# A Mamba block and a binarized feed-forward on one core: decay factors first in each chunk, shifts of the norms on GpSimd, the feed-forward norm on ScalarE, statistics at other places, one bank place skipped

## The chip, the cores and the metric

The kernel runs on one core of a Trainium2 chip. The metric is the device time of one execution in microseconds (us). A core has four compute engines with a queue of instructions each, executed in order: TensorE (PE in the rows), VectorE (DVE), ScalarE (ACT) and GpSimd (POOL). SyncE (SP) issues the DMAs. The engines wait for each other with semaphores only.

## The reference

The input is 8 sequences (batches) of 1024 tokens with 256 features. All in float32:

```
x = x + layernorm(ssd(layernorm(x)))
x = x + layernorm(ffn(layernorm(x)))

ssd:  x, z = in @ Wx.T, in @ Wz.T                    (256 -> 512)
      x = silu(causal_conv(x, 4 taps) + conv_b)
      b, c = x @ Wb.T, x @ Wc.T                      (512 -> 8 heads of 64)
      dt = softplus(x @ Wdt.T + b_dt);  a = -exp(log_a)
      state = exp(dt*a)*state + dt*b (outer) x;  y = c . state     (over 1024 tokens)
      y = y + d_param * x
      yn = (y - mean) / sqrt(var + eps) * gn_w + gn_b   (mean, var per head, over all 1024 tokens)
      out = (yn * silu(z)) @ Wout.T                  (512 -> 256)
ffn:  h = gelu(in @ bw1.T + b1);  out = h @ bw2.T + b2   (256 -> 1024 -> 256)
      bw = mean(|w|) per row * sign(w)
```

## The kernel before

**Staging.** Each batch is two halves (`j` = 0, 1) of 512 tokens, and a half is four chunks (`q` = 0 to 3) of 128. The recurrence is done chunk by chunk. Since the head norm needs the mean over all 1024 tokens, the rest of a batch (head norm, Wout, feed-forward: the "tail") can start only when its second half is through. It is then done inside the next batch: a turn of the loop holds a batch's own steps, the tail of the batch before, and the first steps of the next one.

**Order.** `turn_steps` (from line 147) is one list of steps that all engines share. Each engine walks down the list and issues what the step means for it; steps without a handler on an engine are passed over. So the list sets the order in every queue. After the last batch, `last_tail` orders what is left.

**A half in steady state.** TensorE does the x projection (`xi`), the z projection (`z`), the Wout product of the batch before (`Wo`), then `B`, `dt`, `C` interleaved with the feed-forward of the batch before (`uT` turns its input, `H` is the first layer in eight parts), and then four chunks. VectorE does the convolution and splits float32 tensors into two float16 parts (high part by ScalarE, low part by VectorE: `xh`, `sh`, `uh`, `hh`).

**A chunk** has these steps. `ends`: a matmul gives the decay exponents (key `E`), ScalarE takes the exponential into `Cd`, GpSimd multiplies by `C` (line 814). `front`: exponents of the decay matrix (`seg`), turned x and B (`X`, `Bt`), VectorE makes `xdt` and GpSimd `xdw` (line 807). `score`: C times B, masked by VectorE (`mt`, line 1238). `carry`: the new part of the state (`St`, line 1616) and what the old state gives to y (line 1625); GpSimd scales the state (line 825), VectorE adds to it (line 1244). `back`: the rest of y (line 1638), added by VectorE to `yT` (line 1254). Of the tail, the chunks also carry the second feed-forward layer (`O`), the last norm and the store.

**Norms.** A row norm is: statistics on VectorE (`statistics`, lines 1082 to 1091), 1/sqrt on GpSimd as a power (line 759), and then either one VectorE pass (`normal`, line 1097: the "mid" and "ff" norms) or a shift -mean*rstd on VectorE (line 1109) and a ScalarE pass (line 894: "in" and "end"). The head norm's scale and shift are applied by ScalarE (line 1041, step `gate`); the gate product is VectorE's in the first half and GpSimd's (line 791) in the second. Both `gate` steps of the second half stand in the first half of a turn, behind the step `ff_norm`.

**Banks.** Five of the eight PSUM banks go round among a batch's own products in the order of the list (`Ring`): a matmul waits until the product five places earlier has been read. Two banks serve the tail, one the turned input and the running sums. Every batch starts the round anew at bank 0.

## Time and profile before

| | us |
|---|---|
| median of 3 runs | 1361.92 (1361.39 to 1361.99) |
| profiled execution, its own time | 1363.99 |
| its span, first to last instruction | 1362.2 |
| TensorE / VectorE / ScalarE / GpSimd busy | 92% / 76% / 61% / 34% |
| one turn in steady state | 159.5 |
| mean granted TensorE clock | 0.98 |

The span leaves 1.8 us of the execution's own time outside. One turn is the distance between two equal matmuls a batch apart (483.35 and 642.85 us). A row of the timeline has its start, its length, the engine, the line, the operation with its tensors, and in brackets the idle time before it with the engine that ended it.

### The profile page before, as it was taken

The page shows a single profiled execution, that of the slowest core. Times are in us where ns is not written, and L with a number is a line of the kernel's source. Part 1 is how long each engine was busy: PE and PEld are TensorE (multiplying, and loading weights), DVE is VectorE, ACT ScalarE, POOL GpSimd, SP SyncE. Part 2 cuts the span into 40 slices and gives each one's busy share as a digit, 9 for nine tenths or more (in the row PEclk, how much of TensorE's full clock was granted, in tenths as well). Part 3 has the DMA queues.
Part 4 walks back from the last instruction along what each step waited for, and adds up shares of the span by engine and source line. Part 5 has one row for each costly group of instructions (what it writes and reads, how often), then busy time and mean ns, then how long its engine had stood idle before and what let it go on. Part 6 is the DMA issues. An engine that isn't in the chain of part 4 may idle for free.

```text
span 1362.2 us, 28268 instructions
## 1 busy us (share of the span) xinstructions
PE 1253.5 (92%) x10744; PEld 800.6 (59%) x10744; DVE 1039.2 (76%) x2432; ACT 831.6 (61%) x1432; POOL 458.4 (34%) x527
## 2 busy tenths in 40 slices
PE   6999899999999999999998999999999999989675
PEld 3564657566565756656575665757556475756543
DVE  4664787878879797878978787796977788787574
ACT  5664675657755585656856577565856568565433
POOL 2030433323351334315333243513343153332533
PEclk9998999999999999999999999999999999999888
DMA  7010000101000010100101010010101000000000
GB/s 221 1 48 1 17 0 2 47 1 48 1 18 32 2 47 1 48 1 17 32 2 47 1 48 0 3 47 2 47 2 48 1 2 32 2 32 1 32 1 31
DMA packets 30565, 32.91 MB, mean 24 GB/s; under 512 B 1856, under 2 KB 28628, under 8 KB 30432
## 3 DMA queue, kind: packets, MB, share of 16 engines
q1 hardware_dynamic: 30432, 31.11, 7.1%
q8 instruction: 86, 1.41, 0.4%
q14 instruction: 47, 0.39, 0.1%
HBM read 22.72 MB, written 8.39 MB: 23 GB/s over the span
## 4 chain that ended last, share of the span: by engine, by line
PE 49%; DVE 19%; issue 14%; POOL 12%; ACT 5%; POOLq 0%; DVEq 0%; ACTq 0%
PE bank L1490 21%; PE bank L1675 8%; PE bank L1660 4%; PE bank L1688 4%; DVE xs L1125 4%; POOL Cd L814 3%; PE bank L1602 2%; POOL xdw L807 2%; DVE un L1097 2%; PE bank L1580 2%; DVE hh L1304 2%; DVE gn_stats L1261 1%; POOL state L825 1%; PE bank L1529 1%; POOL y L777 1%
## 5 line engine op out<-in xcount | busy, mean ns | idle before, releaser
L814 POOL TENSOR_TENSOR Cd<-Cd,CT 128x512 f32<-128x512 f32 x64 | 81.2, 1269 | 360.5 <-ACT Cd L1033 360.0
L1490 PE MATMUL bank<-sh,WbT 128*128 128x512 f16 x768 | 177.8, 385 | 12.4 <-DVE sh L1130 12.4
L1490 PE MATMUL bank<-sh,WcT 128*128 128x512 f16 x768 | 175.9, 379 | 0.0
L1490 PEld LDWEIGHTS bank<-sh,WbT 128*128 128x128 f16 x768 | 72.9, 99 | 103.7 <-DVE sh L1130 22.1
L1125 DVE SCALAR_TENSOR_TENSOR xs<-xi,vectors,xs 128x512 f32<-128x512 f32 x168 | 125.2, 749 | 4.5 <-ACT xs L938 0.8
L1490 PEld LDWEIGHTS bank<-sh,WcT 128*128 128x128 f16 x768 | 75.1, 98 | 86.6
L1675 PE MATMUL bank<-uh,sign1T 128*128 128x512 f16 x512 | 121.8, 383 | 2.5 <-DVE uh L1332 2.5
L1062 ACT ACTIVATE hf<-bank,vectors,alpha 128x512 f32<-128x512 f32 x128 | 99.6, 778 | 39.2 <-PE bank L1675 28.0
L1688 PE MATMUL bank<-sign2T,hh 128*128 128x256 f16 x1024 | 119.0, 275 | 1.8 <-DVE hh L1345 1.8
L999 ACT ACTIVATE CT<-bank 128x512 f32<-128x512 f32 x64 | 38.1, 595 | 134.1 <-PE bank L1490 134.1
L1688 PEld LDWEIGHTS bank<-sign2T,hh 128*128 128x128 f16 x1024 | 99.6, 99 | 19.0 <-issue 4.3
L1023 ACT ACTIVATE mt<-bank 128x512 f32<-128x512 f32 x128 | 69.6, 599 | 60.9 <-PE bank L1572 60.9
L1490 PE MATMUL bank<-xh,WxT 128*128 128x512 f16 x384 | 90.5, 388 | 13.5 <-DVE state L1244 13.5
L1343 DVE TENSOR_SCALAR hh<-hf 128x512 f16<-128x512 f32 x128 | 54.4, 425 | 58.4 <-ACT hf L1062 57.9
L1238 DVE TENSOR_TENSOR mt<-bank,mt 128x512 f32<-128x512 f32 x128 | 82.2, 684 | 16.0 <-PE bank L1602 16.0
L759 POOL TENSOR_TENSOR rstd_mid<-var_eps_mid,power 128x4 f32<-128x4 f32 x16 | 16.5, 1034 | 230.7 <-DVE var_eps_mid L1091 230.7
L1345 DVE SCALAR_TENSOR_TENSOR hh<-hf,hh 128x512 f16<-128x512 f32 x128 | 89.0, 695 | 4.4
L807 POOL TENSOR_TENSOR xdw<-xdt,decays 128x512 f32<-128x512 f32 x64 | 66.7, 1042 | 71.5 <-DVE xdt L1229 71.5
L1033 ACT ACTIVATE Cd<-bank 128x512 f32<-128x512 f32 x64 | 38.1, 596 | 83.1 <-PE bank L1591 82.5
L1490 PE MATMUL bank<-xh,WzT 128*128 128x512 f16 x384 | 87.3, 384 | 0.0
L1675 PEld LDWEIGHTS bank<-uh,sign1T 128*128 128x128 f16 x512 | 49.3, 99 | 61.0 <-issue 4.9
L1602 PE MATMUL bank<-CT,BT 64*128 64x128 f32 x1024 | 75.0, 286 | 1.6 <-ACT mt L1023 1.6
(207 smaller groups left out, 2682.4 us busy)
## 6 DMA issues: line engine op xcount, KB each, us to landing
xt<-L_attn_input_tensor_dram SPq DMA_DIRECT2D x16, 512.0 KB, 5.0
u<-L_attn_input_tensor_dram SPq DMA_DIRECT2D x16, 512.0 KB, 4.0
out_dram<-u SPq DMA_DIRECT2D x16, 512.0 KB, 3.0
yT<-in_L_ffn_w_dram SPq DMA_DIRECT2D x2, 512.0 KB, 9.6
u<-in_L_ffn_w_dram SPq DMA_DIRECT2D x2, 512.0 KB, 9.5
BT<-in_L_attn_Wx_dram SPq DMA_DIRECT2D x1, 512.0 KB, 4.8
BT<-in_L_attn_Wz_dram SPq DMA_DIRECT2D x1, 512.0 KB, 5.7
zs<-in_L_attn_Wb_dram SPq DMA_DIRECT2D x1, 512.0 KB, 5.6
```

Of the source, the lines that this page charges most:

```text
L807: pool.tensor_tensor(xdw[n % 2][:, :, :], xdt[n % 2][:, :, :], per_head(to_end[:, q, :]), ALU.mult)\
L814: pool.tensor_tensor(Cd[n % 2][:, :, :], Cd[n % 2][:, :, :], CT[:, :, q * P:(q + 1) * P], ALU.mult)\
L1023: nc.scalar.activation(mt[n % 2][:, g].rearrange("p c t -> p (c t)"), bank(t, ("seg", j, q, g))[:, :], ACT.Exp).then_inc(seg_exp.sem, 1)
L1062: nc.scalar.activation(hf[f % 2][:, :], bank(t, ("H", j, f))[:, :], ACT.Gelu, bias=b1_col[:, f:f + 1], scale=alpha1[:, f:f + 1]).then_inc( ...
L1125: nc.vector.scalar_tensor_tensor(out=conv_sum(j, c), in0=xi[:, c, k:k + BLK], scalar=taps[:, c, k:k + 1], in1=conv_sum(j, c), op0=ALU.mult ...
L1238: nc.vector.tensor_tensor(v, bank(t, ("S", j, q, g))[:, :], v, ALU.mult).then_inc(mt_out.sem, 1)
L1345: nc.vector.scalar_tensor_tensor(out=hh[1][:, f, :], in0=hf[f % 2][:, :], scalar=SG, in1=hh[0][:, f, :], op0=ALU.mult, op1=ALU.subtract).t ...
L1490: mm = nc.tensor.matmul(bank(t, key)[:, :], w[i][:, k, cols(m)], v[h][:, k, :], start=(a == 0), stop=(a == len(terms) - 1))
L1602: mm = nc.tensor.matmul(bank(t, key)[:, cols(c)], BT[rows, c, cols(q)], CT[rows, c, cols(q)], start=True, stop=True)
L1660: mm = nc.tensor.matmul(bank(t, key)[:, (i % 2) * D:(i % 2 + 1) * D], yT[:, c, (j * NQ + i) * P:(j * NQ + i + 1) * P], WoutT[:, c, :], sta ...
L1675: mm = nc.tensor.matmul(bank(t, key)[:, :], sign1T[:, k, cols(f)], uh[i][:, k, :], start=(a == 0), stop=(a == len(terms) - 1))
L1688: mm = nc.tensor.matmul(bank(t, key)[:, (i % 2) * D:(i % 2 + 1) * D], hh[p][:, f, cols(i)], sign2T[:, f, :], start=(a == 0), stop=(a == le ...
```

## The change

Seven things change.

1. In a chunk, `ends` of chunk q+1 stands ahead of its `front` (before: behind the `carry` of chunk q).
2. The shift of a norm is computed by GpSimd right behind the power, from -mean, which VectorE now writes. The feed-forward norm gets a shift too.
3. The feed-forward norm's pass moves from VectorE to ScalarE. Only the first batch's input norm moves the other way.
4. The input norm's statistics move from the first chunk to behind `H` 1; its pass moves to behind the first `front`, and the first turning (`xT` 0) ahead of the second `O`.
5. The head statistics of tokens 0 to 255 move from the end of the first half to the second half, behind `H` 3.
6. `end_root` (1/sqrt of the last norm) moves ahead of `ends`, `front` and `score` of the last chunk.
7. In the ring of five banks one place is left empty ahead of the last `carry` of a batch.

```diff
@@ class Ring
+        self.keys = [key for key in keys if key is not None]
...
+            if key is None:
+                continue
@@ turn_steps
-        steps += own(("C", j, 0), ("cums", j)) + tail(("uT", j)) + own(("roles", j), ("skip", j), ("C", j, 1)) + tail(("H", j, 0), ("H", j, 1))
+        steps += own(("C", j, 0), ("cums", j)) + tail(("uT", j)) + own(("roles", j), ("skip", j), ("C", j, 1))
+        steps += tail(("H", j, 0), ("H", j, 1)) + [(who, "in_stat", nj)]
...
-        steps += own(("C", j, 2)) + tail(("H", j, 2), ("H", j, 3))
+        steps += own(("C", j, 2)) + tail(("H", j, 2), ("H", j, 3)) + (own(("head_stat", 0, 0)) if j else [])
...
-        steps += own(("decays", j), ("ends", j, 0), ("front", j, 0)) + [(who, "in_stat", nj)] + tail(("O", j, 0))
+        norm, xT = [(who, "in_norm", nj)], [[(who, "xT", nj, k)] for k in range(KD)]
+        steps += own(("decays", j), ("ends", j, 0), ("front", j, 0)) + ([] if first else norm) + tail(("O", j, 0))
...
-        steps += own(("score", j, 0), ("front", j, 1))
+        steps += own(("score", j, 0), ("ends", j, 1), ("front", j, 1))
...
-        steps += own(("score", j, 1))
-        norm = [(who, "in_norm", nj)]
-        steps += own(("carry", j, 0), ("ends", j, 1)) + (own(("back", j, 0)) + norm if first else norm + tail(("O", j, 1)) + own(("back", j, 0)))
-        steps += own(("front", j, 2)) + [(who, "xT", nj, 0)] + own(("score", j, 2), ("carry", j, 1), ("ends", j, 2))
-        steps += [(who, "xT", nj, 1)] + own(("back", j, 1)) + tail(("end_stat", j)) + own(("front", j, 3), ("score", j, 3)) + tail(("end_root", j))
+        steps += own(("score", j, 1), ("carry", j, 0)) + ([] if first else xT[0]) + tail(("O", j, 1)) + own(("back", j, 0))
+        steps += (norm if first else []) + own(("ends", j, 2), ("front", j, 2)) + (xT[0] if first else [])
+        steps += own(("score", j, 2), ("carry", j, 1)) + xT[1] + own(("back", j, 1)) + tail(("end_stat", j), ("end_root", j))
+        steps += own(("ends", j, 3), ("front", j, 3), ("score", j, 3))
         steps += [(who, "xi", nj, 0)] if j else []
         steps += own(("head_stat", 1, 0)) if j else []
-        steps += own(("carry", j, 2), ("ends", j, 3)) + tail(("end_norm", j, 0), ("end_norm", j, 1)) + own(("back", j, 2))
+        steps += own(("carry", j, 2)) + tail(("end_norm", j, 0), ("end_norm", j, 1)) + own(("back", j, 2))
...
-        steps += [(who, "silu_table")] + own(("carry", j, 3), ("back", j, 3)) + ([] if j else own(("head_stat", 0, 0)))
+        steps += [(who, "silu_table")] + own(("carry", j, 3), ("back", j, 3))
@@ the ring's keys
+            if (who, kind, *at) == ("own", "carry", NJ - 1, NQ - 1):
+                own_keys.append(None)
@@ GpSimd, inverse_root
+                    if w in ln_shift:
+                        pool.wait_ge(*ln_rstd[w].count(t, j + 1))
+                        pool.tensor_tensor(ln_shift[w][:, :], minus_mean[w][:, :], rstd[w][:, :], ALU.mult)\
+                            .then_inc(ln_shifts[w].sem, 1)
@@ ScalarE
+            def ff_norm(t, j):
+                for i in range(NQ):
+                    normal("ff", un, u[j], t, j, i)
@@ VectorE, statistics
+                    nc.vector.tensor_scalar(minus_mean[w][:, :], moments[w][:, :, 0], -1.0, None, ALU.mult)
...
-                nc.vector.scalar_tensor_tensor(out=ln_shift[w][:, :], in0=moments[w][:, :, 0], scalar=-1.0,
...
-            def ff_norm(t, j):
-
-                for i in range(NQ):
-                    normal("ff", t, j, un[:, i, :], u[j][:, i, :], i).then_inc(un_out.sem, 1)
```

**ScalarE, first half of a turn.** `table_in` is the loading of the gelu table, `un` the feed-forward norm's output, `yT` with `gn_scale` the head norm of the second half, `CT` the first C product copied out of its bank, `cum_hi` the running sums' high part, `uh` the turned feed-forward input. Before:

```order
L890 ACTIVATE table_in<-ones 128x1
L1041 ACTIVATE yT<-yT,gn_shift,gn_scale 128x256 x8
L999 ACTIVATE CT<-bank 128x512
L1006 ACTIVATE cum_hi<-bank 128x128
L1057 ACTIVATE uh<-bank 128x512 x2
```

The same place with the change:

```order
L901 ACTIVATE table_in<-ones 128x1
L905 ACTIVATE un<-u,ln_shift_ff,rstd_ff 128x256 x4
L1056 ACTIVATE yT<-yT,gn_shift,gn_scale 128x256 x8
L1014 ACTIVATE CT<-bank 128x512
L1021 ACTIVATE cum_hi<-bank 128x128
L1072 ACTIVATE uh<-bank 128x512 x2
```

Four passes have come in ahead of the eight head-norm passes, and these stand ahead of `CT` and `uh` as before.

**GpSimd, the last two chunks of a half.** `Cd` are the end factors times C, `xdw` the weighted x, `state` the scaling of the state, `rstd_end` and `ln_shift_end` belong to the last norm, `u0` is the sum that is stored. Before:

```order
L807 TENSOR_TENSOR xdw0<-xdt0,decays 128x512
L825 TENSOR_TENSOR state<-state,decays 128x256
L814 TENSOR_TENSOR Cd0<-Cd0,CT 128x512
L807 TENSOR_TENSOR xdw1<-xdt1,decays 128x512
L759 TENSOR_TENSOR rstd_end<-var_eps_end,power 128x4
L825 TENSOR_TENSOR state<-state,decays 128x256
L814 TENSOR_TENSOR Cd1<-Cd1,CT 128x512
L825 TENSOR_TENSOR state<-state,decays 128x256
L782 TENSOR_TENSOR u0<-u0,y2 128x256 x4
```

The same place with the change:

```order
L825 TENSOR_TENSOR Cd0<-Cd0,CT 128x512
L818 TENSOR_TENSOR xdw0<-xdt0,decays 128x512
L836 TENSOR_TENSOR state<-state,decays 128x256
L766 TENSOR_TENSOR rstd_end<-var_eps_end,power 128x4
L770 TENSOR_TENSOR ln_shift_end<-minus_mean_end,rstd_end 128x4
L825 TENSOR_TENSOR Cd1<-Cd1,CT 128x512
L818 TENSOR_TENSOR xdw1<-xdt1,decays 128x512
L836 TENSOR_TENSOR state<-state,decays 128x256 x2
L793 TENSOR_TENSOR u0<-u0,y2 128x256 x4
```

`rstd_end` now stands ahead of both `Cd1` and `xdw1` of the last chunk, and the scaling of the state behind all of them.

**VectorE, from the end of the first half into the second.** `hh` with `yT` is the gated output's low part, `gn_stats` the head statistics, `xs` with `xi` the convolution, `sh` the low part of its result. Before:

```order
L1254 TENSOR_TENSOR yT<-bank,yT 128x2x128 x2
L1261 BN_STATS gn_stats<-yT 128x6 x4
L1304 SCALAR_TENSOR_TENSOR hh<-yT,hh 128x512 x2
L1125 SCALAR_TENSOR_TENSOR xs<-xi,vectors,xs 128x512 x3
L1261 BN_STATS gn_stats<-yT 128x6 x4
L1125 SCALAR_TENSOR_TENSOR xs<-xi,vectors,xs 128x512 x6
L1130 SCALAR_TENSOR_TENSOR sh<-xs,sh 128x512
```

The same place with the change:

```order
L1266 TENSOR_TENSOR yT<-bank,yT 128x2x128 x2
L1316 SCALAR_TENSOR_TENSOR hh<-yT,hh 128x512 x2
L1137 SCALAR_TENSOR_TENSOR xs<-xi,vectors,xs 128x512 x3
L1273 BN_STATS gn_stats<-yT 128x6 x4
L1137 SCALAR_TENSOR_TENSOR xs<-xi,vectors,xs 128x512 x6
L1142 SCALAR_TENSOR_TENSOR sh<-xs,sh 128x512
```

Four statistics instructions have left the stretch ahead of the convolution.

## Rows read from the trace of the kernel before

**Rows 1.** The page's first part: busy time, share of the span, instructions.
```profile
PE 1253.5 (92%) x10744; PEld 800.6 (59%) x10744; DVE 1039.2 (76%) x2432; ACT 831.6 (61%) x1432; POOL 458.4 (34%) x527
```

**Rows 2.** TensorE's waits, whole run: total us, times, longest.
```profile
PE bank L1625 <- DVE yT L1254: 20.2, 14, 1.8
PE bank L1490 <- DVE state L1244: 13.5, 12, 1.8
PE bank L1490 <- DVE sh L1130: 12.4, 15, 1.9
...
PE bank L1500 <- ACT xt L894: 3.9, 7, 2.7
...
PE bank L1625 <- POOL Cd L814: 1.5, 2, 0.8
```

**Rows 3.** Timeline, feed-forward norm in the first half: start, length, [idle before].
```profile
507.51 4.03 ACT L1041 ACTIVATE yT<-yT,gn_shift,gn_scale 128x256 f32<-128x256 f32 x8
...
511.39 1.02 POOL L759 TENSOR_TENSOR rstd_ff<-var_eps_ff,power 128x4 f32<-128x4 f32 x1 [2.81 <-DVE var_eps_ff L1091]
...
512.44 3.01 DVE L1097 TENSOR_SCALAR un<-u,moments_ff,rstd_ff 128x256 f32<-128x256 f32 x4 [0.53 <-POOL rstd_ff L759]
...
514.24 0.60 ACT L999 ACTIVATE CT<-bank 128x512 f32<-128x512 f32 x1 [2.71 <-PE bank L1490]
...
514.74 0.27 ACT L1006 ACTIVATE cum_hi<-bank 128x128 f16<-128x128 f32 x1
...
515.87 1.08 ACT L1057 ACTIVATE uh<-bank 128x512 f16<-128x512 f32 x2 [0.87 <-PE bank L1500]
...
516.50 1.29 DVE L1332 TENSOR_TENSOR uh<-bank,uh 128x512 f16<-128x512 f32 x2 [0.19 <-ACT uh L1057]
...
518.70 1.89 PE L1675 MATMUL bank<-uh,sign1T 128*128 128x512 f16 x8
```

**Rows 4.** Timeline, the same norm in the second half.
```profile
592.78 1.38 DVE L1097 TENSOR_SCALAR un<-u,moments_ff,rstd_ff 128x256 f32<-128x256 f32 x4 [0.53 <-POOL rstd_ff L759]
...
594.17 1.04 PE L1500 MATMUL bank<-ident,un 128*128 128x128 f32 x8
```

**Rows 5.** Timeline, last two chunks of a first half.
```profile
555.17 0.17 DVE L1091 TENSOR_SCALAR var_eps_end<-moments_end 128x4 f32<-128x4 f32 x1
...
556.05 1.04 POOL L807 TENSOR_TENSOR xdw<-xdt,decays 128x512 f32<-128x512 f32 x1 [3.37 <-DVE xdt L1229]
...
557.05 1.02 POOL L759 TENSOR_TENSOR rstd_end<-var_eps_end,power 128x4 f32<-128x4 f32 x1
...
558.04 0.61 POOL L825 TENSOR_TENSOR state<-state,decays 128x256 f32<-128x256 f32 x1
558.61 1.26 POOL L814 TENSOR_TENSOR Cd<-Cd,CT 128x512 f32<-128x512 f32 x1
...
559.92 2.08 ACT L894 ACTIVATE y<-y,ln_shift_end,rstd_end 128x256 f32<-128x256 f32 x4 [2.26 <-DVE ln_shift_end L1109]
560.33 0.67 PE L1625 MATMUL bank<-Cd,state 64*64 64x128 f32 x16 [1.81 <-DVE yT L1254]
```

**Rows 6.** Timeline, a GpSimd instruction of 128x4 that is no power.
```profile
1.50 0.10 POOL L734 MEMSET power<- 128x4 f32 x1
```

**Rows 7.** Timeline: B in batch 0, x projection after a second half, B later.
```profile
109.91 4.05 PE L1490 MATMUL bank<-sh,WbT 128*128 128x512 f16 x9 [1.94 <-DVE sh L1130]
...
483.35 4.06 PE L1490 MATMUL bank<-xh,WxT 128*128 128x512 f16 x18 [1.76 <-DVE state L1244]
...
579.78 0.82 PE L1490 MATMUL bank<-sh,WbT 128*128 128x512 f16 x3 [0.80 <-DVE sh L1130]
```

**Rows 8.** Timeline, first feed-forward layer of two halves in the last tail.
```profile
1310.23 8.75 PE L1675 MATMUL bank<-uh,sign1T 128*128 128x512 f16 x32 [2.47 <-DVE uh L1332]
...
1332.49 7.07 PE L1675 MATMUL bank<-uh,sign1T 128*128 128x512 f16 x32
```

**Rows 9.** Stretch of TensorE alone: us, busy, granted clock, DMA share, GB/s.
```profile
1310.00:1314.00 4.00, 3.77 (x10) 0.57 0.00 0
```

More of the change, by code:

```diff
@@ L354, in mamba_sandwich_kernel @@
         rstd = {w: sb(f"rstd_{w}", [P, NQ]) for w in LNS}
-        ln_shift = {w: sb(f"ln_shift_{w}", [P, NQ]) for w in ("in", "end")}
+        ln_shift = {w: sb(f"ln_shift_{w}", [P, NQ]) for w in ("in", "ff", "end")}
+        minus_mean = {w: sb(f"minus_mean_{w}", [P, NQ]) for w in ln_shift}
         gn_stats = sb("gn_stats", [P, KI, NJ * 2, 6])
@@ L482, in mamba_sandwich_kernel @@
         ln_rstd = {w: Signal(sem(f"ln_rstd_{w}"), NJ) for w in LNS}
-        ln_shifts = {w: Signal(sem(f"ln_shifts_{w}"), NJ) for w in ("in", "end")}
+        ln_shifts = {w: Signal(sem(f"ln_shifts_{w}"), NJ) for w in ln_shift}
         xn_made = Signal(sem("xn_made"), NJ * NQ)
@@ L540, in mamba_sandwich_kernel @@
         o_out = Signal(sem("o_out"), NJ * NQ)
-        normed = {"in": xn_made, "end": y2_norm}
+        normed = {"in": xn_made, "ff": un_out, "end": y2_norm}
         def ffn_buffer(t, j):
@@ L890, in table, with normal @@
                 return lambda t: nc.scalar.activation(table_in[:, :], ones[:, 0:1], func)
[L892 removed]
+            def normal(w, out, v, t, j, i):
                 act.wait_ge(*ln_shifts[w].count(t, j + 1))
[L894 removed]
+                nc.scalar.activation(out[:, i, :], v[:, i, :], ACT.Identity, bias=ln_shift[w][:, i:i + 1],
                                      scale=rstd[w][:, i:i + 1]).then_inc(normed[w].sem, 1)
             def input_norm(t, j):
+                for i in range(0 if opening(t) else NQ):
+                    normal("in", xt[j], xt[j], t, j, i)
+            def ff_norm(t, j):
                 for i in range(NQ):
[L899 removed]
+                    normal("ff", un, u[j], t, j, i)
             def end_norm(t, j, m=None):
                 for i in range(NQ) if m is None else range(2 * m, 2 * m + 2):
[L903 removed]
+                    normal("end", ffn_buffer(t, j), ffn_buffer(t, j), t, j, i)
             def input_high(t, j, k):
@@ L1102, in input_stats, with input_norm @@
                            lambda i: dve.wait_ge(*x_in[j].count(t, 1)) if i == 0 else None)
-            def shift(w):
-                def step(t, j, m=0):
-                    if m:
-                        return
-                    dve.wait_ge(*ln_rstd[w].count(t, j + 1))
-                    nc.vector.scalar_tensor_tensor(out=ln_shift[w][:, :], in0=moments[w][:, :, 0], scalar=-1.0,
-                                                   in1=rstd[w][:, :], op0=ALU.mult, op1=ALU.mult).then_inc(ln_shifts[w].sem, 1)
-                return step
+            def input_norm(t, j):
+                for i in range(NQ if opening(t) else 0):
+                    normal("in", t, j, xt[j][:, i, :], xt[j][:, i, :], i).then_inc(xn_made.sem, 1)
             def input_low(t, j, k):
@@ L1412, in _ @@
                 "gn_fold": head_fold, "gate": gate, "gated": gated_low, "mid_stat": middle_stats, "mid_norm": middle_norm,
-                "ff_stat": ff_stats, "ff_norm": ff_norm, "uT": middle_low, "H": hidden_split, "O": ffn_out,
-                "end_stat": end_stats, "end_norm": shift("end")}
+                "ff_stat": ff_stats, "uT": middle_low, "H": hidden_split, "O": ffn_out,
+                "end_stat": end_stats}
             dve.wait_ge(masks_made, MASKS_MADE)
```

18 lines of the change are left out of this document (7 added, 11 removed).

## The prediction

> **What bounds the kernel now.** I read the page's busy shares first [rows 1]. TensorE is busy 92% of the span, VectorE 76%, and TensorE goes through the same work every 159.5 us. So what counts is TensorE's idle time, and an edit is worth what it takes from that or adds to it. Next come TensorE's waits [rows 2]. Three stand out: the last chunk's old-state product waits for VectorE's addition into `yT` (20.2 us in 14 halves, up to 1.81 [rows 5]); the x projection waits for VectorE's state addition (13.5; 1.76 after each second half [rows 7]); B waits for the low part `sh` (12.4). They add up to 46 us, and that is about the most that the change can win. Last I followed the timeline around each moved step.
>
> **1. The feed-forward norm on ScalarE, first half.** Before, ScalarE does eight head-norm passes from 507.51 to 511.54, in time in which it has nothing else to do, and then idles 2.71 us until C's first bank is full at 514.24 [rows 3]. Now the four norm passes stand ahead of these eight. They need the shift, which comes after the power that ends at 512.41. With -mean on VectorE (0.1) and the shift (0.2, below) they start at about 512.8. Four passes take 2.08 us [rows 5], the eight 4.03, the copy of C 0.5 to its successor, `cum_hi` 0.27 and the two copies of `uh` 1.08 [rows 3]. The copies end at 512.8 + 2.1 + 4.05 + 0.5 + 0.27 + 1.08 = 520.8. VectorE's low part ended 0.84 behind ScalarE (517.79 against 516.95), so 521.65, and the hidden layer starts at 521.8 instead of 518.70: +3.1 us. TensorE meanwhile has only the turning of `un` and one C product, which were through at 518.70 before and would be a little earlier now, since ScalarE's last pass ends at 514.9 and VectorE's ended at 515.45. So it stands idle for over 3.1, some 3.5 us in one piece. Seven turns: +21.7.
>
> **2. The clock after that idle time.** Before the hidden layer of the last tail TensorE idles 2.47 us; the 32 matmuls then take 8.75 us, where the same 32 take 7.07 at full speed [rows 8], and the granted clock of that stretch is 0.57, so most of it ran at 1.2 instead of 2.4 GHz [rows 9]. After the 1.81 us waits nothing of the kind shows: that product has its usual 0.67 [rows 5]. A pause of 3.5 us lies beyond the 2.47. I take the measured 1.68 each time, seven times +11.8. Bounds 0 and 1.7.
>
> **3. The same norm, second half.** No head-norm passes stand in the way. VectorE needed 1.38 us for the four parts and TensorE began to turn them at 594.17 without a wait [rows 4]. ScalarE takes 2.08 and starts about 0.3 later (-mean, shift), so the last part is there at 595.3 and the turning ends 0.8 later. +0.8 seven times: +5.6. In the first half VectorE's passes took 3.01 us [rows 3], beside GpSimd's gate products; that gain is in part 1, where it only makes the pause longer.
>
> The Trainium skill (VectorE: DVE Perf Modes, "Mode 2×_2P — use both read ports for one tensor") says that a float32 operation with one tensor source in SBUF runs two elements per cycle on VectorE, which speaks against moving this pass. By that rule VectorE's four passes are the cheaper ones; the rows (1.38 against 2.08) agree, and the sum has their difference already.
>
> **4. The shift on GpSimd.** No row shows a small product on GpSimd. Below it lies a memset of the same 128x4 at 0.10 [rows 6], above it the power at 1.02 [rows 5]. I take 0.2 with its wait, near the memset, since the scaling of a whole 128x256 state takes only 0.61. VectorE loses its own shift between the state addition and the addition into `yT`.
>
> The Trainium skill (GPSIMD Engine Reference, "2.1 Instruction dispatch") gives an indirect call of tens of cycles per instruction; an estimate from that page is under 0.1 us, and the sum would be lower by about 2 us.
>
> **5. End of a half.** The wait of 1.81 does not go, it changes its reason. GpSimd's queue before: `xdw` (1.04), power (1.02), state (0.61), `Cd` [rows 5]. Now: power, shift, `Cd` (1.26), `xdw` (1.04), state. The queue starts when the variance is there (555.34 before; 555.7 now, with one more small VectorE operation in front, a slightly later start and the semaphore), so state scaling runs at 555.7 + 1.02 + 0.25 + 1.27 + 1.04 = 559.3 to 559.9 instead of 558.04 to 558.65. VectorE adds until 560.4, and the product that started at 560.33 starts at 560.5. Queued behind `Cd` is `xdw` of the last chunk, needed by the last `St`, which waits for it until 559.3 too, inside the same pause. In the second half it is the same with head statistics in between: about +0.3 for VectorE's state and `yT` additions. The early `ends` adds another thing: in chunk 1, `X` now comes five places behind the first `score` bank and waits for VectorE's mask, 0.1 us a half. Fourteen halves: +1.4 for both together.
>
> **6. What really goes.** After the first half VectorE is ahead: the last norm's pass starts on ScalarE some 2.5 us earlier (at 557.0 instead of 559.92 [rows 5]), hence also the gated output, and the head statistics of four instructions are gone from here. Of the x projection's 13.5, six waits of 1.76 are 10.6 and the first batch has some 0.8; the rest, 2.1, lies after first halves and goes: -2.1. The waits of B in second halves go too: of the 12.4 some 5.1 are the first batch's, whose waits are the long ones (1.94 [rows 7]) and stay; -7.3. After the second half the skipped place frees the first x product of the 1.76 wait, but its second one takes the bank of `St`, whose reader is the same state addition behind the convolution, and then the head means wait for statistics that come 0.3 later. I give it -0.2 in six turns, -1.2; bounds 0 and -10.6.
>
> **7. First batch and last tail.** Without a tail, the early end factors and early norm work as meant: of the waits for `xt` (3.9), for `Cd` (1.5) and one of 0.8 for the state I let 5.8 go, -5.8. In the last tail one ScalarE norm and two shifts lie open: +1.0.
>
> The statistics of the input norm go into VectorE's pauses between the hidden parts; they take some 2.2 us a half (four statistics, four aggregates, two small operations); VectorE is not what TensorE waits for there, and if the pauses did not hide them, the hidden parts would come up to 2.2 later in a half, before a second layer that starts only after the first `front`. The DMAs wait for the same steps as before.
>
> **Sum.** 21.7 + 11.8 + 5.6 + 1.4 - 2.1 - 7.3 - 1.2 - 5.8 + 1.0 = +25.1. On the profiled execution (1362.2 of span and 1.8 around it, 1364.0) that is 1389.1; this one is 2.1 above the median of the runs, so for a run like those it is 1361.9 + 25.1 = 1387.
>
> **Rivals.**
> A. The pause does not pull the clock down, or only in part. For it: the pause sits between dense matmuls, while the last tail is thin anyway. Against it: [rows 8, 9]. 1387 - 11.8 = 1375. Chance 0.15.
> B. A small GpSimd product costs nearly what the power costs, 0.8 more than I took. It lies in both feed-forward norms and both ends of a half, four times a turn: +22, 1409. For it: every 128x4 operation between tensors there has 1.02. Chance 0.08.
> C. Faster: the ends of the halves come free. If the variance of the last norm reaches GpSimd before the last chunk's `Cd` and `xdw` are wanted, the state chain runs as early as TensorE allows, and most of the 20.2 (18.4) and the rest of the 1.76 (9.4) go, with the 1.4 of part 5. 1387 - 29 = 1358. It decides at a power done by 554.5 instead of 556.7. For it: 1.8 us of VectorE work (shifts, input statistics) has left the chunks. Against it: VectorE's end statistics stand behind the addition of chunk 1, which TensorE's `back` sets. Chance 0.09.
> D. ScalarE's stall comes out shorter, because VectorE is relieved in the half and the chain of the norm runs ahead: 2 us earlier makes it +1.1 without a clock drop, and 1387 - 14 - 11.8 = 1361, no change. Against it: that chain (B's second bank, step sizes, statistics) is paced by TensorE, not by VectorE. Chance 0.04.
> The forecast keeps 0.64.
>
> **Range and chances.** Within 0.2% (2.7 us) is about what a measurement of this kernel cannot tell from no change. The forecast and A, with unknown costs at their bounds, hold 1366 to 1400. This leaves out C, D and the far end of B, under 0.2 together. Slower: forecast, A and B, 0.87; faster: C, 0.09; same: D, 0.04.
>
> **What would show it.** Right: in the first half of a turn ScalarE's eight head-norm passes run at a time when C's bank is already full, TensorE waits over 3 us for `uh` at the hidden layer, seven times, with a granted clock below 1 behind it; `St` of the last chunk waits for `xdw`; B's waits in second halves are gone. Wrong: the head-norm passes ahead of the norm, a shift of 1 us on GpSimd, or the old-state product of the last chunk without a wait.

## The result, and the profile after

The changed kernel takes 1391.99 us (median of 4 runs, 1385.13 to 1392.88) against 1361.95: ratio 1.0209, 95% interval 1.0176 to 1.0243. It is slower, and by 5 us more than predicted. The page's busy shares, which answer to [rows 1]:

```profile
PE 1280.5 (92%) x10744; PEld 810.1 (58%) x10744; DVE 983.7 (71%) x2392; ACT 850.3 (61%) x1488; POOL 475.3 (34%) x575
```

VectorE is busy 55 us less, as the moves intend. TensorE does the same 10744 matmuls and is busy 27 us longer, while its idle time has hardly grown (108.7 and 109.0, span less busy). Its clock has fallen. The listing of cores (span, mean granted clock), first of the kernel before, then of the changed one:

```profile
core 0: 1362.2 us, clock 0.980
```
```profile
core 0: 1389.5 us, clock 0.964
```

Span times mean clock is what the span would be if every low stretch were at full speed: 1335.0 and 1339.5. (The clock's last digit is worth 1.4 us. A low stretch over TensorE's idle time counts too, though it costs nothing, so these two numbers give the clock too large a part. Where it matters I use what the low clock takes from TensorE's busy time in the trace: 18.5 us before and 36.7 now.) The medians over the runs are 1336.7 before and 1338.9 after; the time lost to low clock is 24.5 and 51.4. I call these two numbers "at full clock" and "lost to the clock" below.

TensorE's waits of the changed kernel, which answer to [rows 2]:

```profile
PE bank L1682 <- DVE uh L1339: 23.1, 8, 3.0
PE bank L1623 <- POOL xdw L818: 13.2, 14, 1.4
PE bank L1507 <- ACT un L905: 6.8, 11, 5.2
PE bank L1497 <- DVE sh L1142: 6.7, 4, 1.9
PE bank L1652 <- DVE gn_mom L1285: 6.7, 8, 3.1
...
PE bank L1632 <- DVE yT L1266: 5.1, 8, 0.7
PE bank L1632 <- DVE state L1256: 2.9, 7, 0.4
PE bank L1497 <- DVE state L1256: 2.2, 6, 0.4
```

The three long entries of before have shrunk from 46 us to 14 (6.7, 5.1, 2.2). In their place stand 23.1 us for `uh` (seven times 3.02, once in the last tail) and 13.2 for `xdw`. The first of them, in the turn of [rows 3]:

```profile
513.53 0.20 POOL L770 TENSOR_TENSOR ln_shift_ff<-minus_mean_ff,rstd_ff 128x4 f32<-128x4 f32 x1
513.77 2.07 ACT L905 ACTIVATE un<-u,ln_shift_ff,rstd_ff 128x256 f32<-128x256 f32 x4 [5.18 <-POOL ln_shift_ff L770]
515.75 4.03 ACT L1056 ACTIVATE yT<-yT,gn_shift,gn_scale 128x256 f32<-128x256 f32 x8
519.68 0.57 ACT L1014 ACTIVATE CT<-bank 128x512 f32<-128x512 f32 x1
520.15 0.26 ACT L1021 ACTIVATE cum_hi<-bank 128x128 f16<-128x128 f32 x1
520.31 1.06 ACT L1072 ACTIVATE uh<-bank 128x512 f16<-128x512 f32 x2
520.92 1.29 DVE L1339 TENSOR_TENSOR uh<-bank,uh 128x512 f16<-128x512 f32 x2
522.27 3.23 PE L1682 MATMUL bank<-uh,sign1T 128*128 128x512 f16 x8 [3.02 <-DVE uh L1339]
```

ScalarE idles 5.18 us, then the norm and eight head-norm passes stand in one row ahead of C, `cum_hi` and `uh`. The first eight matmuls of the hidden layer wait 3.02 us and take 3.23, against 1.89 before [rows 3]. The end of the same first half, GpSimd and then TensorE, against [rows 5]:

```profile
560.96 1.02 POOL L766 TENSOR_TENSOR rstd_end<-var_eps_end,power 128x4 f32<-128x4 f32 x1 [4.07 <-DVE var_eps_end L1107]
562.05 0.20 POOL L770 TENSOR_TENSOR ln_shift_end<-minus_mean_end,rstd_end 128x4 f32<-128x4 f32 x1
562.21 1.28 POOL L825 TENSOR_TENSOR Cd<-Cd,CT 128x512 f32<-128x512 f32 x1
563.44 1.04 POOL L818 TENSOR_TENSOR xdw<-xdt,decays 128x512 f32<-128x512 f32 x1
564.44 0.62 POOL L836 TENSOR_TENSOR state<-state,decays 128x256 f32<-128x256 f32 x1
...
564.63 0.69 PE L1623 MATMUL bank<-xdw,bt 128*64 128x64 f32 x16 [1.42 <-POOL xdw L818]
565.73 0.97 PE L1632 MATMUL bank<-Cd,state 64*64 64x128 f32 x16 [0.41 <-DVE state L1256]
566.62 1.98 PE L1645 MATMUL bank<-mt,xdt 128*64 128x128 f32 x16
```

The old-state product takes 0.97 where it took 0.67 [rows 5], and the `back` product behind it 1.98, against 1.09 in the same turn of the kernel before. Windows of TensorE (length, busy, granted clock) show both places; the first window is the hidden layer of the first turn, which starts at 195.68 after the same wait of 3.02:

```profile
195.00:199.00 4.00, 3.32 (x16) 1.00 0.00 0
522.00:526.00 4.00, 3.73 (x12) 0.63 0.00 0
565.00:569.00 4.00, 3.59 (x45) 0.62 0.02 4
```

Going through the whole trace in windows of 2 us, every stretch of low clock that stands alone adds up to the same 1.7 us lost. Inside the seven turns the changed kernel has 13 of them: behind the wait for `uh` in six turns of seven, and behind the waits for `xdw` and the state at the end of the first half in all seven. Those behind `uh` begin 0.5 to 0.8 us before the matmuls do, so the matmuls lose only 1.3 to 1.5 (they take 3.22 to 3.35 instead of 1.90). The kernel before has 2, and they stand behind the single wait of 1.81 us that [rows 5] shows, in two of its seven turns:

```profile
241.32 0.67 PE L1625 MATMUL bank<-Cd,state 64*64 64x128 f32 x16 [1.81 <-DVE yT L1254]
241.92 1.82 PE L1638 MATMUL bank<-mt,xdt 128*64 128x128 f32 x16
```

The old-state product itself still has its 0.67 there. Only the `back` product behind it, 1.82 here and 1.65 at 880.02, shows the low clock.

From one head-mean product to the next, a steady turn went from 159.5 to 163.85 us, and seven of them, the shorter last one included, from 1113.1 to 1144.0. The first batch ends 6.8 us earlier, the last tail is 3.2 longer: -6.8 + 30.9 + 3.2 = 27.3, the difference of the spans. The 30.9 of the turns are 3.9 of idle time (52.4 and 56.3), 18.0 of low clock over TensorE's busy time (3.4 and 21.4), and 9.0 of busy time at full clock (1057.2 and 1066.2). The last part is spread thinly. Its largest piece is the old-state product: where the product of the decay exponents stood behind it, in five chunks of a turn it held TensorE for 0.49 us, and now, with other products behind it, for 0.60 (read in e6 below, whose turns have no low clock).

### The profile page after: what moved, and what is told of

It reads as the page before. It is cut to its first block, busy times and chain, and to the rows that moved or that the text cites. A ratio compares the mean times of both kernels' runs of the same rounds, so it can differ in the third digit from the quotient of the medians.

```text
span 1389.5 us, 28357 instructions
## 1 busy us (share of the span) xinstructions
PE 1280.5 (92%) x10744; PEld 810.1 (58%) x10744; DVE 983.7 (71%) x2392; ACT 850.3 (61%) x1488; POOL 475.3 (34%) x575
## 3 DMA queue, kind: packets, MB, share of 16 engines
q8 instruction: 86, 1.41, 0.4%
## 4 chain that ended last, share of the span: by engine, by line
PE 61%; DVE 19%; POOL 7%; issue 7%; ACT 6%; DVEq 0%; POOLq 0%; ACTq 0%
PE bank L1497 18%; PE bank L1682 8%; PE bank L1695 8%; PE bank L1667 4%; PE bank L1609 4%; PE bank L1663 3%; PE bank L1587 3%; ACT yT L1056 3%; PE bank L1645 2%; PE bank L1632 2%; PE bank L1579 2%; DVE un L1113 2%; DVE yT L1266 2%; PE bank L1623 1%; ACT un L905 1%
## 5 line engine op out<-in xcount | busy, mean ns | idle before, releaser
L1682 PE MATMUL bank<-uh,sign1T 128*128 128x512 f16 x512 | 128.3, 398 | 23.1 <-DVE uh L1339 23.1
L1077 ACT ACTIVATE hf<-bank,vectors,alpha 128x512 f32<-128x512 f32 x128 | 99.1, 777 | 37.5 <-PE bank L1682 28.6
L1250 DVE TENSOR_TENSOR mt<-bank,mt 128x512 f32<-128x512 f32 x128 | 82.3, 684 | 36.1 <-PE bank L1609 36.1
L766 POOL TENSOR_TENSOR rstd_in<-var_eps_in,power 128x4 f32<-128x4 f32 x16 | 18.6, 1164 | 213.3 <-DVE var_eps_in L1107 213.3
L905 ACT ACTIVATE un<-u,ln_shift_ff,rstd_ff 128x256 f32<-128x256 f32 x64 | 33.2, 589 | 88.0 <-POOL ln_shift_ff L770 88.0
L1056 ACT ACTIVATE yT<-yT,gn_shift,gn_scale 128x256 f32<-128x256 f32 x128 | 65.1, 587 | 25.2 <-DVE gn_shift L1304 25.2
L1645 PE MATMUL bank<-mt,xdt 128*64 128x128 f32 x1024 | 77.1, 297 | 0.0
```

What stands on the lines that cost most here:

```text
L1056: nc.scalar.activation(v, v, ACT.Identity, bias=gn_shift[:, c:c + 1], scale=gn_scale[:, c:c + 1]).then_inc(yn_out.sem, 1)
L1077: nc.scalar.activation(hf[f % 2][:, :], bank(t, ("H", j, f))[:, :], ACT.Gelu, bias=b1_col[:, f:f + 1], scale=alpha1[:, f:f + 1]).then_inc( ...
L1250: nc.vector.tensor_tensor(v, bank(t, ("S", j, q, g))[:, :], v, ALU.mult).then_inc(mt_out.sem, 1)
L1645: mm = nc.tensor.matmul(bank(t, key)[g * HD:(g + 1) * HD, cols(c // 2)], xdt[r][:, c * HP + g, :], mt[r][:, side(c * HP + g), c, :], start ...
L1682: mm = nc.tensor.matmul(bank(t, key)[:, :], sign1T[:, k, cols(f)], uh[i][:, k, :], start=(a == 0), stop=(a == len(terms) - 1))
```

## The experiments

All ratios are to the kernel before, run beside each kernel on the same chip; "full" and "lost" are the medians of the two numbers explained above. Beside e9, e10 and e11 the kernel before itself read 1339.1 and 21.8, not 1336.7 and 24.5, so "full" and "lost" of these three compare with the others only to some 3 us. The last two columns are from each kernel's trace and hold the seven turns alone: TensorE's idle time, and what low clock took from its busy time. What is left of the turns, busy time at full clock, is 1057.2 us before, 1059.1 in e3, and 1063.8 to 1068.5 in every kernel that keeps most of the new order.

| kernel | us | ratio, 95% | full | lost | idle in turns | low in turns |
|---|---|---|---|---|---|---|
| before | 1361.95 | 1 | 1336.7 | 24.5 | 52.4 | 3.4 |
| changed | 1391.99 | 1.0209 (1.0176 to 1.0243) | 1338.9 | 51.4 | 56.3 | 21.4 |
| e1 head-norm passes first | 1357.68 | 0.9960 (0.9948 to 0.9973) | 1319.4 | 36.6 | 35.6 | 8.0 |
| e2 half of them first | 1360.91 | 0.9985 (0.9970 to 1.0001) | 1332.6 | 26.5 | 43.4 | 3.4 |
| e3 before + norm on ScalarE | 1399.99 | 1.0270 (1.0238 to 1.0303) | 1357.5 | 40.5 | 70.8 | 19.5 |
| e4 changed, old last chunk | 1376.89 | 1.0109 (1.0086 to 1.0133) | 1343.0 | 31.6 | 56.8 | 9.6 |
| e5 changed, norm on VectorE | 1354.41 | 0.9933 (0.9916 to 0.9949) | 1321.4 | 31.1 | 37.5 | 5.1 |
| e6 = e1, power behind xdw | 1344.43 | 0.9863 (0.9848 to 0.9877) | 1320.0 | 22.8 | 33.0 | 0.0 |
| e7 = e1, no place skipped | 1360.63 | 0.9977 (0.9966 to 0.9988) | 1326.2 | 32.6 | 40.1 | 10.2 |
| e8 = e1, head statistics back | 1354.69 | 0.9934 (0.9920 to 0.9949) | 1323.2 | 29.8 | 36.5 | 4.1 |
| e9 = e1, input statistics back | 1350.26 | 0.9913 (0.9899 to 0.9928) | 1322.4 | 26.3 | 36.1 | 3.4 |
| e10 = e1, power behind state | 1343.87 | 0.9863 (0.9849 to 0.9878) | 1320.0 | 22.1 | 30.5 | 0.0 |
| e11 = e5, power behind xdw | 1344.60 | 0.9875 (0.9859 to 0.9892) | 1316.4 | 26.2 | 33.6 | 0.0 |
| e12 = e11, input statistics back | 1341.16 | 0.9836 (0.9822 to 0.9849) | 1316.3 | 24.1 | 33.7 | 0.0 |

**e1: the head-norm passes ahead of the norm.**

```
-        steps += own(("B", j, 2)) + tail(("ff_norm", j))
+        steps += own(("B", j, 2)) + (tail(("gate", 1, 0), ("gate", 1, 1)) if j == 0 else []) + tail(("ff_norm", j))
...
-        steps += tail(("gate", 1, 0), ("gate", 1, 1)) if j == 0 else []
```

> The changed kernel with one thing moved: on ScalarE (and on VectorE and GpSimd with it) both head-norm steps of the second half's gate (eight passes, 4.03 us) stand ahead of the feed-forward norm. My theory: the eight passes behind the norm cause the 3.02 us stall of the first hidden product in seven turns, and the stall causes the low clock behind it (3.23 us for eight matmuls instead of 1.89). Both go, at most 0.3 us of stall stays: (3.0 - 0.2 + 1.35) x 7 = 29 us less than the changed kernel's 1392, about 1363, ratio to the kernel before 1.00. Rival: the norm is late because its chain through GpSimd (power, shift) is late and the passes only fill that wait; then the order of the passes gives less than 5 us: above 1387.

Its timeline at the same place:

```profile
498.74 4.03 ACT L1055 ACTIVATE yT<-yT,gn_shift,gn_scale 128x256 f32<-128x256 f32 x8
...
504.02 2.08 ACT L904 ACTIVATE un<-u,ln_shift_ff,rstd_ff 128x256 f32<-128x256 f32 x4 [1.26 <-POOL ln_shift_ff L769]
...
509.35 1.89 PE L1681 MATMUL bank<-uh,sign1T 128*128 128x512 f16 x8
```

The passes are through before the shift is there, the norm starts as early as it can, and the hidden layer starts without a wait. 34 us less than the changed kernel, nearly all of it inside the turns: 20.7 of idle time and 13.4 of low clock. The rival is refuted.

**e2: only four of the eight passes ahead.** As e1, with `("gate", 1, 0)` alone in front.

> The changed kernel with only the first of the two head-norm steps (four of the eight passes, 2.0 us) moved ahead of the feed-forward norm. It separates the stall from the clock. Stall: 3.0 - 2.0 = about 1.0 us, -14 us in seven turns by every theory. My theory: a pause of about 1 us does not pull the clock down, so the first hidden product takes 1.89 again instead of 3.23: another 1.35 x 7 = 9.4 less, together 1392 - 23 = 1369. Rival: any pause of 1 us there lowers the clock as much: 1378, with 3.2 us for the first eight matmuls.

```profile
513.06 1.90 PE L1682 MATMUL bank<-uh,sign1T 128*128 128x512 f16 x8 [1.06 <-DVE uh L1339]
```

A pause of 1.06 us leaves the clock alone in all seven turns; 3.02 did not. The time is 8 us below my 1369. At the ends of first halves, too, only two stretches of low clock are left of seven, though the waits there are the same 1.42 and 0.41, and five stretches of 1.7 us are about these 8. Nothing in my theory says why they went; I come back to it.

**e3: the kernel before with that one part.** The norm on ScalarE and its shift on GpSimd:

```
...
+            def ff_norm(t, j):
+                for i in range(NQ):
+                    act.wait_ge(*ln_shifts["ff"].count(t, j + 1))
+                    nc.scalar.activation(un[:, i, :], u[j][:, i, :], ACT.Identity, bias=ln_shift["ff"][:, i:i + 1],
+                                         scale=rstd["ff"][:, i:i + 1]).then_inc(un_out.sem, 1)
...
```

> The kernel before with one part of the change alone: the feed-forward norm runs on ScalarE with its shift on GpSimd, where it stood on VectorE; all else as before. My theory: this part alone costs more than the whole change, since it carries the stall (3.1 us), the low clock behind it (1.35 as the changed kernel shows) and 0.8 us in the second half: 5.2 x 7 = 37 us over 1362, about 1399, minus what VectorE's relief gives back (up to 6): 1393 to 1399. Rival: the stall and the clock need the other parts (later ends of chunks, statistics of the next norm between the hidden parts): then it is under 1380.

```profile
528.54 3.59 PE L1683 MATMUL bank<-uh,sign1T 128*128 128x512 f16 x8 [3.02 <-DVE uh L1340]
```

The same 3.02 without any other edit, and 2.7% or 37 us slower than the kernel before beside it; the 1399.99 lies just above the range that I gave. This part alone costs more than the whole change. It also has low clock behind the 1.81 us wait at the end of the first half in four turns of seven, where the kernel before has it in two.

**e4: the last chunk in its old order.**

```
-... + tail(("end_stat", j), ("end_root", j))
-        steps += own(("ends", j, 3), ("front", j, 3), ("score", j, 3))
+... + tail(("end_stat", j))
+        steps += own(("front", j, 3), ("score", j, 3)) + tail(("end_root", j))
...
-        steps += own(("carry", j, 2)) + tail(("end_norm", j, 0), ...
+        steps += own(("carry", j, 2), ("ends", j, 3)) + tail(("end_norm", j, 0), ...
```

> The changed kernel with the last chunk of each half in its old order (the end norm's power behind the last score, the last end factor behind the last state product's step). In the changed kernel the last state product of the first half waits 1.42 us for xdw and the old-state product 0.41 for the state, and the granted clock behind them is 0.62; the delay against the kernel before grows by 1.5 us there, and by 0.6 at the end of the second half. My theory: the new order of GpSimd's queue (power, shift, Cd, xdw, state) makes this, so the old one gives back 2.1 x 7 = 15 us: about 1377, and the clock there is 1.00 again although one wait of about 1.8 us for yT returns. Rival: VectorE's last additions set the end of the half anyway and the waits only change their names: 1389 to 1395.

```profile
560.04 0.63 PE L1623 MATMUL bank<-xdw,bt 128*64 128x64 f32 x16
562.55 0.67 PE L1632 MATMUL bank<-Cd,state 64*64 64x128 f32 x16 [1.88 <-POOL Cd L825]
563.14 1.09 PE L1645 MATMUL bank<-mt,xdt 128*64 128x128 f32 x16
```

The time is what I wrote, but not for the whole reason that I gave. Inside the turns TensorE idles as long as in the changed kernel (56.8 and 56.3); what the old order gives back is low clock, 9.6 us of it where there were 21.4. A wait of 1.88 (here for `Cd`, not for `yT`) leaves `back` at 1.09 in six turns and is followed by low clock in one; 1.42 and 0.41 with a short product between were followed by it in all seven. Behind the unchanged wait of 3.02 for `uh` there are five low stretches instead of six.

**e5: the norm back on VectorE, all else changed.**

```
...
+            def ff_norm(t, j):
+
+                for i in range(NQ):
+                    normal("ff", t, j, un[:, i, :], u[j][:, i, :], i).then_inc(un_out.sem, 1)
...
```

> The changed kernel with one part undone: the feed-forward norm is on VectorE again, as in the kernel before; all else stays changed. My theory: the norm's move alone is what makes the change slow (stall 3.2 us, low clock 1.35, second half 0.8, together 5.3 x 7 = 37 us), so this is 1392 - 37 = 1355, 0.5% faster than the kernel before. Rival: VectorE, which takes 3.0 us for the four passes in the first half and 1.4 in the second, is late again for the low parts and the statistics that the change has put between the hidden parts; then waits of TensorE for VectorE come back and it is 1362 to 1370.

1354.4: undoing that one part turns 2% slower into 0.7% faster. TensorE's wait for the turning of `un` is 0.40 in first halves and none in second ones. No wait for VectorE's low parts comes back.

**e6: the power behind `Cd` and `xdw`, on top of e1.**

```
-... + tail(("end_stat", j), ("end_root", j))
-        steps += own(("ends", j, 3), ("front", j, 3), ("score", j, 3))
+... + tail(("end_stat", j))
+        steps += own(("ends", j, 3), ("front", j, 3), ("score", j, 3)) + tail(("end_root", j))
```

> The kernel with the head-norm passes first (1357.7) and in the last chunk of each half one more move: the end norm's power stands behind the chunk's Cd and xdw on GpSimd, where the changed kernel has it ahead of both. In the changed kernel GpSimd stands idle for 4.07 us ahead of the power and then runs power, shift, Cd (1.27), xdw (1.04), state back to back while TensorE waits 1.42 for xdw and 0.41 for the state, and after that in 3 to 7 halves has a stretch of low clock that costs 1.7 us each. My theory: Cd goes into the idle time, the last state product no longer waits, the state comes about 1 us earlier: 1.2 us less in a first half, 0.5 in a second, no low clock: 12 + 5 = 17 less, 1341. Rival: xdw needs VectorE's xdt, which comes behind the variance, so the power is 1.3 us later and the state with it; the wait for the state takes the place of the wait for xdw: 1353 to 1360.

GpSimd and TensorE at the end of a first half:

```profile
541.68 1.28 POOL L824 TENSOR_TENSOR Cd<-Cd,CT 128x512 f32<-128x512 f32 x1 [1.94 <-ACT Cd L1047]
544.41 1.04 POOL L817 TENSOR_TENSOR xdw<-xdt,decays 128x512 f32<-128x512 f32 x1 [1.45 <-DVE xdt L1240]
545.41 1.02 POOL L765 TENSOR_TENSOR rstd_end<-var_eps_end,power 128x4 f32<-128x4 f32 x1
...
546.66 0.61 POOL L835 TENSOR_TENSOR state<-state,decays 128x256 f32<-128x256 f32 x1
```
```profile
547.94 0.67 PE L1631 MATMUL bank<-Cd,state 64*64 64x128 f32 x16 [1.40 <-DVE state L1255]
```

13.3 us less, and neither theory is wholly right. The wait for `xdw` is gone and one of 1.40 for the state stands in its place, as the rival says; idle time inside the turns falls by 2.6 only. But this pause pulls no clock down in any turn, and that is worth 8.0 us of the 10.6 by which the turns got shorter. The pause is both in one piece and shorter than the 1.82 of e1, so e6 does not show which of the two saves the clock.

**e7: no bank place skipped, on top of e1.**

```
-            if (who, kind, *at) == ("own", "carry", NJ - 1, NQ - 1):
-                own_keys.append(None)
```

> The kernel with the head-norm passes first (1357.7) without the skipped bank place. In the kernel before the second x product after a second half waits 1.76 us for VectorE's state addition, in the changed one 0.36. My theory, from the prediction: the skipped place is worth 0.2 us in six turns, the rest of that wait has gone since GpSimd and VectorE end the half earlier: +1, 1356 to 1361. Rival: the skipped place alone took the wait away; without it 1.4 us come back in six turns: +8.4, 1366.

```profile
478.46 4.06 PE L1494 MATMUL bank<-xh,WxT 128*128 128x512 f16 x18 [2.02 <-DVE state L1253]
```

The 2.02 us wait is back, against 0.36 in e1. Most of it had only changed its name: e1 waits 0.51 for the head means, 0.70 instead of 0.41 before the old-state product, and 0.25 instead of 0.15 before the output projection. The time at full clock is 6.8 us higher, the idle time inside the turns 4.5, the time 3 us. The skipped place is worth 3 to 7 us, not the 1.2 that I gave it, and not the rival's 8.4.

**e8 and e9: which edit took B's waits away?** e8 puts the head statistics back at the end of the first half, e9 the input statistics and the input norm back into the chunks, each on top of e1:

```
-... tail(("H", j, 2), ("H", j, 3)) + (own(("head_stat", 0, 0)) if j else [])
+... tail(("H", j, 2), ("H", j, 3))
...
-... own(("carry", j, 3), ("back", j, 3))
+... own(("carry", j, 3), ("back", j, 3)) + ([] if j else own(("head_stat", 0, 0)))
```
```
-        steps += tail(("H", j, 0), ("H", j, 1)) + [(who, "in_stat", nj)]
+        steps += tail(("H", j, 0), ("H", j, 1))
...
-        steps += own(("decays", j), ("ends", j, 0), ("front", j, 0)) + ([] if first else norm) + tail(("O", j, 0))
+        steps += own(("decays", j), ("ends", j, 0), ("front", j, 0)) + [(who, "in_stat", nj)] + tail(("O", j, 0))
...
```

> The kernel with the head-norm passes first (1357.7) with the head statistics of the first half back at that half's end on VectorE, where the change has put them between the hidden parts of the second half. My theory, from the prediction: those four instructions made VectorE late for the low parts of the second half; TensorE's waits of 0.8 and 0.5 us for them ahead of B come back seven times, net 1.0: +7, 1365. Rival: the waits are gone because the shifts and the input statistics left the chunks; then the move costs under 2 us: below 1360.

> The kernel with the head-norm passes first (ratio 0.996 to the kernel before) with the input statistics and the input norm back in their old places inside the chunks. It asks once more why the waits of B for sh in the second halves are gone (0.8 and 0.5 us a turn in the kernel before), now that the head statistics are found not to be the reason. First theory: 2.2 us of statistics out of VectorE's chunks let it end the half sooner; with them back the waits return, +1.0 x 7 = 7: 1362 to 1366, ratio 1.001. Rival: TensorE ends the first half 0.8 us later than in the kernel before, by the wait for xdw, and that hides them; the move itself costs under 2 us, ratio below 0.998.

TensorE's waits for `sh` in e9; e8's line reads the same:

```profile
PE bank L1496 <- DVE sh L1141: 6.7, 4, 1.9
```

Neither brings a wait back; both are the first batch's. My reason fell twice. What does bring one back is a shorter end of the first half: in e6 B waits 0.30 again in the second half, in e10 0.48. So a part of these waits went because TensorE itself arrives later. The rest is open. Both kernels are faster than e1, with nearly the same waits (35.6, 36.5 and 36.1 us of idle time in the turns); what differs is the low clock there, 8.0, 4.1 and 3.4, from four stretches, two and two.

**e10: the power behind the state's scaling too.** On top of e6:

```
-... ("score", j, 3)) + tail(("end_root", j))
+... ("score", j, 3))
...
-        steps += own(("carry", j, 2)) + tail(("end_norm", j, 0), ...
+        steps += own(("carry", j, 2)) + tail(("end_root", j), ("end_norm", j, 0), ...
```

> The kernel with the head-norm passes first and the end norm's power behind the scaling of the state too (Cd, xdw, state, power on GpSimd); the kernel with Cd, xdw, power, state took 1344.4. There the old-state product of the last chunk waits 1.40 us for the state in first halves and 0.59 for yT in second ones, and the power and the shift are the 1.2 us ahead of the state's scaling. My theory: the state comes 1.2 us sooner in first halves, and the end norm, which ScalarE then starts 0.6 us later, holds nobody up: 1344.4 - 7 x 1.2 = 1336. In second halves nothing changes. Rival: ScalarE's norm delays the gated copies and the x copies behind it, or VectorE's last additions are late by themselves: 1343 to 1348.

```profile
546.81 0.67 PE L1631 MATMUL bank<-Cd,state 64*64 64x128 f32 x16 [0.15 <-DVE state L1255]
...
552.32 2.76 PE L1496 MATMUL bank<-xh,WxT 128*128 128x512 f16 x12 [1.11 <-DVE state L1255]
567.45 1.47 PE L1496 MATMUL bank<-sh,WbT 128*128 128x512 f16 x6 [0.48 <-DVE sh L1141]
```

The 1.40 is down to 0.15, as planned, and 1.11 comes back at the second x product. It needs VectorE's next state addition, and that is queued behind the low part of the gated output, which waits for ScalarE's copy behind the later end norm:

```profile
549.42 1.13 ACT L1063 ACTIVATE hh<-yT 128x512 f16<-128x512 f32 x2
550.07 1.86 DVE L1315 SCALAR_TENSOR_TENSOR hh<-yT,hh 128x512 f16<-128x512 f32 x2 [2.73 <-ACT hh L1063]
```

The time is the rival's.

**e11 and e12: the two repairs together, then the statistics in their old place.** e11 is e5 with e6's edit of the last chunk; e12 adds e9's edit:

```
...
+        steps += own(("ends", j, 3), ("front", j, 3), ("score", j, 3)) + tail(("end_root", j))
...
+        steps += own(("decays", j), ("ends", j, 0), ("front", j, 0)) + [(who, "in_stat", nj)] + tail(("O", j, 0))
...
```

> The changed kernel with two parts undone or mended: the feed-forward norm on VectorE as in the kernel before, and the end norm's power behind Cd and xdw. The same on ScalarE, with the head-norm passes first, took 1344.4 (ratio 0.9863). If the two repairs add up (1354.4 for the norm on VectorE; 1344.4 - 1357.7 = -13.3 for the power): 1341, ratio 0.984. Rival: without the wait at the first half's end TensorE comes sooner to the second half, where VectorE now has 1.4 us of norm passes more, and waits of B and of the turning of un for VectorE return: 1346 to 1352.

> The changed kernel with the feed-forward norm on VectorE, the end norm's power behind Cd and xdw, and the input statistics and input norm back in their old places. Without the last of the three it took 1344.6 (ratio 0.9875). With the head-norm passes first, taking the statistics back gave 1357.7 to 1350.3, though no wait of TensorE changed; span times mean clock, the span as it would be at full speed, stayed at 1322.3 and 1321.4, so I read that gain as fewer stretches of low clock. If so: here span times clock stays at 1317 within 2, there are no stretches of low clock inside the turns to lose any more, and the time is 1340 to 1346, ratio 0.985 to 0.988. Rival: the old place of the statistics is better by itself, by 5 us or more: under 1339, with span times clock under 1314. Third: now that the ends of the first halves have no wait for xdw, VectorE's 2.2 us of statistics a half make its low parts late for B: over 1348.

e11 misses its 1341 by 3.6 us; of the rival's waits a small one came (0.31 for B). e12 is the fastest kernel of all, 1341.16 us, 1.6% below the kernel before. Its time at full clock is e11's, as expected, and the medians of the time lost to the clock are 2.1 us apart. But neither trace has a low stretch inside the turns, and these take the same time (1097.9 and 1097.5 us), so where the 3.4 us between the two come from is not shown.

## Why the prediction was right, and where it was only lucky

The forecast was 1387 for 1392. Its largest term held; that the sum came so close is luck. For the turns it had 29.9 us: 11.8 of clock and 18.1 of all else. They measured 30.9: 18.0 of clock and 12.9 of all else, and 9.0 of the latter is busy time for which the forecast had no term.

1. **ScalarE's stall**: right. 3.02 us for 3.1, in all seven turns; e1, e2 and e3 show the cause from three sides. In e1 the idle time of the turns fell by 20.7, for 21.7.
2. **The clock behind it**: right in mechanism, too large in size. It came in six turns and not seven, and cost TensorE 1.3 to 1.5 us each time, since the low stretch begins in the pause: 8.1 for 11.8. Rival A is out.
3. **The norm in second halves**: the step "the turning ends 0.8 later" was too large. With the stall out of the way, ScalarE against VectorE is -1.6 us over the seven turns in one pair (e1, e5) and 1.3 in the other (e6, e11), low clock taken out, not 5.6. ScalarE's passes overlap TensorE's turning part by part: TensorE waits 0.16 there.
4. **The shift on GpSimd**: 0.20, exactly what I took between the memset and the power; no row had shown it, so the exact hit is luck. Rival B is out. The Trainium skill (VectorE: DVE Perf Modes, "Mode 2×_2P — use both read ports for one tensor") says that this mode gives two float32 results per cycle where one tensor is read, which speaks for VectorE. The rows agree (1.38 for four passes [rows 4] against 2.07 on ScalarE), but the passes' own price was the small part, the queue that they joined was the large one.
5. **End of a half**: the failed step. GpSimd's queue came out as worked out (the state's scaling starts 3.48 us after the power does, 3.58 in my schedule). But "inside the same pause" was wrong twice. The last `St` stands ahead of the old-state product in TensorE's queue, so TensorE now pauses ahead of `St` and again behind it. And the waits at the ends shrank more than I allowed. Inside the turns, those for `yT`, for the state, ahead of `xs` and ahead of the output projection were 35.8 us before (20.2, 12.7, 2.3, 0.6). Now, with those for `xdw` and the head means that came up in their place, they are 28.4 (`xdw` 13.2, the state 5.1, `yT` 4.9, the head means 3.5, the output projection 1.7). That is -7.4, where parts 5 and 6 have -2 for it. Against that stand seven stretches of low clock, some 12 us, which I had not foreseen at all. I had read [rows 5] as proof that a pause of this size is harmless. It is no proof even for the kernel before: behind the same 1.81 us its clock fell in two turns of seven, and the product whose 0.67 I quoted doesn't show it, the next one does. Those two stretches did not lengthen their turns (159.49 and 159.53 us, as the others).
6. **B's waits**: the 7.3 in the turns went, as forecast; the first batch's grew from 5.1 to 6.7. The reason that I gave is refuted by e8 and e9.
7. **First batch and last tail**: -6.8 for -5.8. The tail is 3.2 for 1.0, with more low clock in it.

Rival C, the free ends, decided on a power done by 554.5; what holds it up is not the power's place, since e6 and e10 move it and the wait only moves along the chain from GpSimd's state to VectorE's addition. No kernel here got the ends free.

## What to carry to other kernels

Before a pass is moved to an idle engine, look at what stands behind it in that engine's queue: here ScalarE was idle before the norm's input was ready and full after it, and changing the order of two steps was worth 34 us. Look at the time lost to the clock apart from the waits: two edits here (e4, e9) changed TensorE's idle time in the turns by 0.5 us and the time by 15 and 7 us. And one harmless pause in the rows does not make its size harmless: go through every turn, and look at the products behind the one that waited. Whether one pause is better than the same pause in two pieces is not shown here, since no two runs differ in that alone. The counts of low stretches lean that way: 24 of 49 turns for 1.4 and 0.4 us with a short product between (changed, e1, e2, e5, e7, e8, e9), 7 of 21 for one pause of 1.8 to 1.9 at the same place (before, e3, e4), none of 21 for one of 1.4 (e6, e11, e12).

## What was not expected of the hardware

Pauses of the same length don't always have the same effect. Behind 3.02 us TensorE's eight matmuls took 1.90 in the first turn and 3.22 to 3.35 in the six others. In e1 the same two pauses at the end of a first half (1.41 and 0.41) come with low clock in one turn and without in another, the turn before it in the same trace:

```profile
392.17 0.69 PE L1622 MATMUL bank<-xdw,bt 128*64 128x64 f32 x16 [1.41 <-POOL xdw L817]
393.27 0.67 PE L1631 MATMUL bank<-Cd,state 64*64 64x128 f32 x16 [0.41 <-DVE state L1255]
393.87 1.09 PE L1644 MATMUL bank<-mt,xdt 128*64 128x128 f32 x16
...
550.37 0.69 PE L1622 MATMUL bank<-xdw,bt 128*64 128x64 f32 x16 [1.41 <-POOL xdw L817]
551.46 0.86 PE L1631 MATMUL bank<-Cd,state 64*64 64x128 f32 x16 [0.41 <-DVE state L1255]
```

There the changed kernel has low clock in all seven turns, e1 and e7 in four, e5 in three, e2, e8 and e9 in two, with the same waits; an edit elsewhere in the turn changes how often the clock falls. Executions of one kernel differ too: the four of the changed one took 1385.13 to 1392.88 us and lost 42.9 to 52.9 to the clock. The Trainium skill (TensorE: Matmul & The Clock Gate, "What's actually happening") says that how many matmuls run slowly varies from run to run of one kernel; it says so of the kernel's start, and these four agree for its middle. What decides in the single case no run here settles.
